# Moving the FFN gate's Exp and its VectorE step forward in the bodies of a software-pipelined conv, attention and FFN kernel

## The reference, cut to what matters

```
x = x + leaky_relu( sum over the top 2 of 5 experts of gate * (GN(x) @ We + be) )     # the "conv"
t = tokens(x)
t = t + attention(LN(t))          # 6 heads of 16, causal, 256 tokens an image
t = t + FFN(LN(t))                # 4 experts, 96 -> 384 -> 96, erf GELU, top 2 by a softmax gate
```

## Time and profile before

| | |
|---|---|
| median of 3 runs | 435.12 us (433.81 to 436.12) |
| profiled execution, first to last instruction | 430.4 us |
| PE busy | 348.9 us (81%) |
| DVE busy | 264.2 us (61%) |
| ACT busy | 217.2 us (50%) |
| POOL busy | 101.7 us (24%) |

### The profile page before, as it was taken

One profiled execution on the slowest core, in us unless ns is written; L12 is line 12 of the kernel. 1 busy time (PEld: TensorE's weight loads), 2 busy tenths in 40 slices (PEclk: granted clock), 3 DMA queues, 4 the chain that ended last, 5 costly groups with the idle time before them and its releaser, 6 DMA issues.

```text
span 430.4 us, 8037 instructions
## 1 busy us (share of the span) xinstructions
PE 348.9 (81%) x2536; PEld 268.5 (62%) x2536; DVE 264.2 (61%) x933; ACT 217.2 (50%) x383; POOL 101.7 (24%) x133
## 2 busy tenths in 40 slices
PE   4522754959888999998999993998999979988975
PEld 3411522536567867775787673884977578757765
DVE  5885248436866887586668662794778664514231
ACT  3530322533884379347935870359547932691540
POOL 8341400540143024202420432004400520031000
PEclk9765565796999999999999996999999998999999
DMA  8500420060004001500160023000510040000000
GB/s 177 112 0 0 83 28 2 3 110 0 3 4 108 2 2 29 104 0 4 31 100 0 5 62 68 0 2 0 101 28 2 1 123 7 4 21 0 2 18 20
DMA packets 23930, 14.69 MB, mean 34 GB/s; under 512 B 14145, under 2 KB 23893, under 8 KB 23894
## 3 DMA queue, kind: packets, MB, share of 16 engines
q1 hardware_dynamic: 23894, 14.27, 16.6%
HBM read 3.10 MB, written 1.57 MB: 11 GB/s over the span
## 4 chain that ended last, share of the span: by engine, by line
PE 57%; DVE 11%; SPq 9%; issue 8%; ACT 5%; DMA 5%; POOL 2%; DVEq 0%; POOLq 0%; ACTq 0%
PE PS L715 17%; PE PS L656 8%; SPq L416 7%; PE PS L658 6%; PE PS L657 6%; PE PS L812 4%; DMA k_stack<-qk_parts 3%; ACT prob_a L629 3%; PE PS L772 2%; PE PS L732 2%; PE PS L793 2%; DVE mixed L1045 2%; DVE result L1014 2%; PE PS L759 2%; PE PS L768 1%
## 5 line engine op out<-in xcount | busy, mean ns | idle before, releaser
L715 PEld LDWEIGHTS PS<-w_f,hidden 128*128 128x128 f32 x768 | 93.2, 198 | 0.1
L715 PE MATMUL PS<-w_f,hidden 128*128 128x96 f32 x768 | 93.1, 279 | 0.0
L577 ACT ACTIVATE hidden<-PS 128x512 f32<-128x512 f32 x96 | 56.5, 597 | 54.0 <-PE PS L658 51.7
L1082 DVE TENSOR_REDUCE row_max<-PS 128x2 f32<-128x512 f32 (+2 forms) x80 | 48.4, 635 | 36.3 <-PE PS L763 25.3
L498 POOL TENSOR_TENSOR ln_var<-ln_mv,eps_t 128x4 f32<-128x4 f32 x16 | 3.2, 198 | 179.4 <-DVE ln_mv L979 179.4
L656 PE MATMUL PS<-t_hi,w_hi 128*128 128x512 f32 x96 | 44.5, 463 | 0.6 <-DVE t_lo L1061 0.5
L658 PE MATMUL PS<-t_hi,w_lo 128*128 128x512 f32 x96 | 38.4, 400 | 0.0
L657 PE MATMUL PS<-t_lo,w_hi 128*128 128x512 f32 x96 | 38.2, 398 | 0.0
L987 DVE TENSOR_SCALAR normed<-res,ln_mv,ln_scale 128x96 f32<-128x96 f32 x64 | 22.6, 415 | 25.0 <-POOL ln_scale L501 25.0
L1014 DVE SCALAR_TENSOR_TENSOR result<-PS,weight,result 128x96 f32<-128x96 f32 x96 | 23.7, 309 | 19.0 <-PE PS L715 19.0
L586 ACT ACTIVATE conv_y<-PS 128x486 f32<-128x486 f32 x32 | 18.5, 577 | 27.6 <-PE PS L658 26.5
(11 more groups left out here) (173 smaller groups left out, 731.2 us busy)
## 6 DMA issues: line engine op xcount, KB each, us to landing
q_stack<-qk_parts SPq DMA_DIRECT2D x48, 96.0 KB, 3.2
k_stack<-qk_parts SPq DMA_DIRECT2D x48, 96.0 KB, 3.7
out_dram<-result SPq DMA_DIRECT2D x8, 192.0 KB, 2.9
X<-in_x_dram SPq DMA_DIRECT2D x3, 384.0 KB, 4.8
w_f<-in_L_ffn_w_dram SPq DMA_DIRECT2D x2, 576.0 KB
X<-in_x_dram SPq DMA_DIRECT2D x2, 192.0 KB, 2.8
conv_f<-in_L_conv_We_dram SPq DMA_DIRECT2D x1, 180.0 KB
k_stack<-shift_t SPq DMA_DIRECT2D x8, 18.0 KB
```

Of the source, the lines that this page charges most:

```text
L577: act.activation(hidden[:, m, :], PS[:, HIDDEN_BANKS[m % 2], :], ACT.Gelu).then_inc(h_ready, 1)
L715: mm = pe.matmul(dst, hidden[:, m, t * P:(t + 1) * P], w2_f[:, m, :], start=False, stop=t == TILES - 1 and c == CHUNKS - 1, skip_group_che ...
L1082: dve.tensor_reduce(dst, src, AX_X, ALU.max).then_inc(dve_drained[stage], 1)
```

## The change

Only the order table changes. In ScalarE's order the step `gate2` goes from between `pv` 1 and `qk` 1 to right behind the last `prob`, ahead of `norm1_t` and `ffn1` 9. In VectorE's order it goes from between `norm1_t` and `qk` 0 to between `shift` and `mix` 1.

```diff
@@ SCALAR
-        ("prob", 1, 1), ("prob", 1, 2), ("prob", 1, 3), ("prob", 1, 4), ("norm1_t",), ("ffn1", 9), ("pv", 0),
-        ("qk", 0), ("pv", 1), ("gate2",), ("qk", 1), ("ffn1", 10), ("ffn1", 11), ("v",)],
+        ("prob", 1, 1), ("prob", 1, 2), ("prob", 1, 3), ("prob", 1, 4), ("gate2",), ("norm1_t",), ("ffn1", 9), ("pv", 0),
+        ("qk", 0), ("pv", 1), ("qk", 1), ("ffn1", 10), ("ffn1", 11), ("v",)],
@@ VECTOR
-        ("shift",), ("mix", 1), ("mix", 2), ("mix", 3), ("mix", 4), ("stats1",), ("norm1",), ("norm1_t",),
-        ("gate2",), ("qk", 0), ("ffn2", 3), ("out_t", 0), ("out_t", 1), ("qk", 1), ("weights",)],
+        ("shift",), ("gate2",), ("mix", 1), ("mix", 2), ("mix", 3), ("mix", 4), ("stats1",), ("norm1",), ("norm1_t",),
+        ("qk", 0), ("ffn2", 3), ("out_t", 0), ("out_t", 1), ("qk", 1), ("weights",)],
```

## The result

| | before | after |
|---|---|---|
| median of 4 runs each | 434.47 us (432.74 to 436.12) | 457.81 us (454.77 to 460.74) |
| ratio, 95% interval | | 1.0533 (1.0466 to 1.0599) |
| profiled execution, span | 430.4 us | 453.1 us |
| granted clock, mean of the span | 0.911 | 0.879 |

The change costs 5.3%, 23.3 us between the medians and 22.7 us between the two profiled spans. The forecast had the sign and missed the size: 10.3 us, and a range that ended at 449. One remark on what the numbers stand on: each of the four runs of after lies 1.7 us above its own span. The 4.7 us that I put between before's span and the median of the runs were therefore mostly a quick execution, not time outside the span.

A forecast was written before the change was run, and what follows sets the result against it. TensorE was taken to bound the kernel, with VectorE's chain to `normed` late in four of six full bodies. Delays and body 9 summed to 11.05, less 0.7, 10.3 us: 445.4 us, range 443.5 to 449 at 63%.

The forecast's parts named there:

- 1.87 assumed for each: VectorE's gate step ahead of the mixing: nothing covers it, so the whole chain to `normed` gets 1.87 us later.
- the bodies that I named: TensorE's wait for `normed` at L732: 2 us or so in bodies 2, 3, 5 and 7, under 1 in 4 and 6.
- Body 9's load: Body 9, ScalarE: Gelu's table load runs after the wait for TensorE, making Gelu 9 late, +1.29 us (bounds 0 and 1.29).
- the rival on TensorE's clock: Waits of 2 to 3 us ahead of the transposes pull TensorE's clock down: 449 to 452 us, chance 8%.
- the stall of 0.9 us in body 2: Argument against a falling TensorE clock: this stall in body 2 of before left it at full clock.
- the row of a long stall: Argument for a falling TensorE clock: after the loop jump's 8 us stall the granted clock is 0.62 for 6 us.
- the delay that I forecast: Later start of TensorE's transposes of `norm1_t`, bodies 2 to 7: 0.55 to 2.4 us each, 9.8 in sum.
- I take the 2.64 of body 2: `normed` on VectorE beside GpSimd's selects running back to back: 2.64 us for 4, as in body 2 of before.
- The upper bound: `normed` on VectorE: 4 x 0.87 = 3.48 us if each of the four had to wait out a select.
- the cover of 2.7 us: Bodies 4 and 6: `normed` ends 2.7 us ahead of the transposes, leaving a delay of 0.55 us each (bounds 0 and 0.8).
- -0.7 forecast: Gain from ScalarE's missing loads: 0.49 us behind the loop jump and about 0.23 at the loop's entry, -0.7 in all.
- the stacks hang on `qk` 0: The copy of `qk` 0 is ahead of the loads that go, so the stacks gain nothing and move with the transposes.

The follow-up runs named there:

- e1: The changed kernel with ScalarE's order as before, so only VectorE's gate step moves: 456.81 us, ratio 1.0511.
- e6: e4 with ScalarE's gate step at its old place in the bodies without attention, so body 9 is that of before: 435.01 us, ratio 1.0007.
- e7: e6 with VectorE's step split: the four Exp instructions in the wait for the root, the ranking behind the transposes: 434.62 us, ratio 1.0004.
- e3: The changed kernel with eight matmuls on constants added on TensorE ahead of its wait for `normed`: 450.8 us, ratio 1.039.
- e2: The changed kernel with GpSimd's causal selects cut to one head of six, masking of the other five left out: 438.16 us, ratio 1.0087.
- e9: e7 with the four Exp instructions of the gate step ahead of the mixing, the ranking at its old place: 441.42 us, ratio 1.012.
- e8: e7 with GpSimd's first select of a body waiting until `normed` is done: 433.16 us, ratio 0.9972.
- e4: The changed kernel with VectorE's gate step between the statistics and `normed`, in the wait for GpSimd's root: 435.84 us, ratio 1.0062.

## Why the prediction was wrong in size

**Right.** Apart from body 9, ScalarE's order costs and gives nothing that can be measured (e1, e6, e7). The gate step ahead of the mixing is hardly covered: it begins at 248.90 in body 5 and mixing at 250.88, 1.98 us, and counted from `shift_t` the start of `normed` moves by 1.87 and 1.88 us in bodies 2 and 3, 2.22 and 2.24 in 4 and 6, 1.60 and 1.63 in 5 and 7, against 1.87 assumed for each. The loss sits at L732 in the bodies that I named, only that body 6 waited 1.62 us there and not under 1. Body 9's load runs after the wait: 1.29 forecast, 1.29 measured, and gone in e6. The Exp started 1.30 us after its load (428.16, 429.46). The Trainium skill (ScalarE: Activation LUTs, What ACT_TABLE_LOAD costs) counts 2.66 us a switch; this trace does not show the drain in it, as before.

**Failed first: the rival on TensorE's clock, at 8% and 1 to 1.5 us a body.** The prediction said "the stall of 0.9 us in body 2 left it at full clock" and concluded from it on waits of 2 to 3 us. That is a row of a wait a third as long; the row of a long stall that I did have the earlier trace rows spoke the other way, and I weighed it as the weaker. The clock fell in five of six bodies and cost 9.3 us of longer stretches, 1.2 to 2.7 a body. What it cost the kernel is not the same: by e3 it is 4.5 us of span, with the extra low stretches of that execution in it, and 6 to 7 of the median. In the ledger this term alone is about as large as the whole of the delay that I forecast. The 1.6 us of body 4 are among the 9.3, though the clock had fallen there ahead of the wait for `normed` (see below).

**Failed second: "I take the 2.64 of body 2".** The upper bound, one select for each of the four `normed`, was the case: 3.23 us in bodies 2, 3, 5, 6 and 7, and 2.63 in body 4. Once the root is late enough, GpSimd's four selects stand in a row behind it, and each `normed` waits for one. The rule that I cited (the Trainium skill, SBUF — State Buffer, Who interferes with whom: the second to issue waits until the first is done) agrees with this trace at its strictest, 0.8 to 0.9 us a `normed` beside selects of 0.86. The 2.64 was a misread row, too. I took it for the price when selects run throughout, but in body 2 of before they did not:

```profile
118.50 0.86 POOL L528 TENSOR_SCALAR_AFFINE_SELECT prob_b<-prob_b 128x768 f32<-128x768 f32 x1
119.48 0.91 POOL L528 TENSOR_SCALAR_AFFINE_SELECT prob_a<-prob_a 128x768 f32<-128x768 f32 x1
```

Between the end of the one at 119.36 and the start of the other GpSimd was free for 0.12 us, and the third `normed` of the four (119.34) took 0.32 us there, the others 0.79, 0.90 and 0.86. So body 2's `normed` could still grow, by 0.6 us. In body 6 the cover of 2.7 us was used up by 2.24 us of a later start and 2.18 of `normed` (3.23 less 1.05): 1.74 late instead of 0.55. Together 13.5 us instead of 9.8, 3.7 us of the miss.

**Given back: -0.7 forecast, -3.8 measured.** Bodies 3, 4 and 6 give back nothing (0.03, 0.01, 0.05 us), as argued: the stacks hang on `qk` 0. Body 5, with the loop's jump behind it, gives back 0.91 against 0.49 forecast. Bodies 2 and 7 give back 0.86 and 1.98, which the forecast had not, and both come from what this execution of before met there. In body 7, the first two lines are before, the last two after:

```profile
355.82 0.39 PE L759 MATMUL PS<-causal_b,ident_b 128*128 128x512 bf16 x1 [3.20 <-DMA k_stack<-qk_parts]
357.10 4.44 PE L715 MATMUL PS<-w_f,hidden 128*128 128x96 f32 x24
378.77 0.39 PE L759 MATMUL PS<-causal_b,ident_b 128*128 128x512 bf16 x1 [2.83 <-DMA k_stack<-qk_parts]
380.05 2.81 PE L715 MATMUL PS<-w_f,hidden 128*128 128x96 f32 x24
```

Before had its own fall of the clock here (0.50 from 357.30 to 360.70, after 1.00): 1.63 us on the same 24 matmuls, and 0.37 us more of waiting. From the transposes of `att_t` in body 7 to the next `shift_t` the four traces without a fall of the clock in between (after, e1, e2, e9) take 26.6 to 27.2 us, the eight with one (before and e3 among them) 28.4 to 32.1. Why some have it and some not is open. In body 2 TensorE waited 0.70 us in before for the last DMAs of k (at 139.75), and in after it did not. The other traces gave this back as well, by 0.72 to 0.87 us (e7: 0.47), e8 too, whose transposes come earlier than before's.

**Outside the change: 2.4 us** ahead of body 2's `shift_t`, where both kernels run the same instructions. Over the twelve profiled kernels, most of which are the same up to there, this point lies between 111.4 and 114.7 us, before at 111.44 and after at 113.84. In this pair it goes with the granted clock of the filling bodies (0.80 and 1.00 against 0.67 and 0.83 in the early stretches above).

So of the 12.4 us by which the span missed the forecast, 9.3 are the stretches at the lower clock, 3.7 the delay (the selects, for the most part), 2.4 the scatter ahead, and -3.1 what was given back besides. Had I taken the upper end of my own bound for `normed`, the delay would have been right within 1 us, and the clock would still have put the time outside the range.

**Open.** Why the clock falls in one body and not in another. In body 4 of after it was already at 0.50 at 213.6, ahead of the wait for `normed` (0.68 us there), behind a wait of 1.12 us for an Exp that before has as well (1.13) at a clock of 1.00; body 6 waits 1.62 us for `normed` and keeps 1.00. In e1 bodies 4 and 6 both wait 1.62 us for `normed`; the clock is 0.50 behind it in the one and 1.00 in the other. The last wait's length alone does not decide. And e8's 0.3% is not shown.

## What to carry to other kernels

Time taken off an engine is worth nothing until one has named who waits for it; here 14 table loads of ScalarE, 18 us, bought nothing that could be measured, and 2 us of VectorE a body, ahead of the chain that TensorE hangs on, cost some 22 (e1). Price such a delay three times over: the step itself, what it newly runs beside (here selects that take turns with VectorE's `normed`; a row of before gives that price only if the two really overlap throughout), and the clock of the TensorE work behind a wait that has grown. A step that must come early belongs into a wait that its engine has anyway: in VectorE's 1.48 us for the root the same instructions cost nothing that could be measured, once body 9's load was out of the way.

## What the runs showed of the hardware that I had not expected

- TensorE's clock was down to 0.50 to 0.72 in stretches of 5 to 6 us behind waits of 1.4 to 3.4 us (after, e2, e4, e9), in body 5 of e2 behind one of 0.69, but stayed at 1.00 behind 1.62 us in body 6 of after, and work at the lower level took up to 1.7 times as long: four transposes 1.09 us instead of 0.64, six `pv` matmuls 1.08 instead of 0.63. In after the stretch behind a wait of 2.5 to 3.4 us was longer by 1.2 to 2.7 us.
- Eight matmuls on constants, 1.89 us that nothing needs, kept the clock at 1.00 in all six stretches and made the kernel 6 to 7 us faster than without them.
- VectorE's [128 x 96] f32 scaling of 0.32 us takes up to 0.90 us beside GpSimd's [128 x 768] select of 0.86, one for one, so whether four of them take 1.05 or 3.23 us is a matter of when GpSimd starts.
